# A fused embedding, SSM and mixture-of-experts block: row norms taken two tiles at a time, GpSimd work in smaller pieces, bias scaling on ScalarE

## The reference

```python
h = embed(ids) * 16                       # four tables, each with its projection to 256
x = layernorm(h)                          # over the 256 channels of a row
x1 = x @ w1.T + b1
xc = silu(depthwise_conv3(x1))            # along the sequence
y  = ssm(xc)                              # h = h*sigmoid(A) + x*B; y = sum(h*C) + D*x
h  = h + (y * silu(x @ v1.T + b2)) @ w2.T + b3
x = layernorm(h)
h = h + (shared_mlp(x) + mean of two hashed experts(x)) / 2
```

## Time and profile before

| | us |
|---|---|
| median of 3 runs | 460.0 (458.8 to 461.04) |
| the profiled execution, whole | 457.65 |
| its span in the profile | 455.8 |
| PE busy, DVE busy | 404.1, 292.9 |
| ACT busy, POOL busy | 240.3, 225.9 |
| stage A (start to first SSM matmul) | 0 to 141.8 |
| stage B (to the last toep slice) | 141.8 to 172 |

### The profile page before, as it was taken

One profiled execution on the slowest core, in us unless ns is written; L12 is line 12 of the kernel. 1 busy time (PEld: TensorE's weight loads), 2 busy tenths in 40 slices (PEclk: granted clock), 3 DMA queues, 4 the chain that ended last, 5 costly groups with the idle time before them and its releaser, 6 DMA issues.

```text
span 455.8 us, 8449 instructions
## 1 busy us (share of the span) xinstructions
PE 404.1 (89%) x2880; PEld 353.5 (78%) x2880; DVE 292.9 (64%) x624; ACT 240.3 (53%) x433; POOL 225.9 (50%) x242
## 2 busy tenths in 40 slices
PE   3778898999688777499899999999999999998996
PEld 3667776888467775278798898888988998987885
DVE  6678999978956568966555556375466465565333
ACT  4556776778477425553553654544535544534442
POOL 6787877952891007562834535535445337244000
PEclk9999999999899889789999999999999999999999
DMA  2324111139299997110130120130130121100101
GB/s 61 116 78 154 47 43 48 52 113 319 77 318 285 221 258 239 47 47 0 47 93 1 47 92 2 46 92 0 46 93 28 40 70 46 47 0 0 47 0 46
DMA packets 32619, 38.86 MB, mean 85 GB/s; under 512 B 3301, under 2 KB 28867, under 8 KB 32464
## 3 DMA queue, kind: packets, MB, share of 16 engines
q1 hardware_dynamic: 29456, 32.99, 24.8%
q0 software_dynamic: 3136, 5.52, 4.1%
HBM read 34.56 MB, written 8.65 MB: 95 GB/s over the span
## 4 chain that ended last, share of the span: by engine, by line
PE 63%; DVE 19%; issue 6%; ACT 5%; DMA 4%; POOL 1%; DVEq 0%; ACTq 0%; SPq 0%; POOLq 0%
PE ps L1128 19%; PE ps L1129 19%; PE ps L1130 19%; DVE hn L953 3%; DMA toep_l<-kernel_rows_dram 3%; DVE hid_lo L1059 3%; PE ps L1211 2%; DVE stat L940 2%; DVE catT_lo L933 1%; PE ps L1247 1%; DVE h2n L953 1%; DVE v_sb L1013 1%; DVE sw_lo L1006 1%; PE ps L1136 1%; PE ps L1166 1%
## 5 line engine op out<-in xcount | busy, mean ns | idle before, releaser
L1059 DVE SCALAR_TENSOR_TENSOR hid_lo<-act_out,hid_hi 128x512 fp32r<-128x512 f32 x64 | 54.5, 853 | 56.4 <-ACT hid_hi L847 56.4
L834 ACT ACTIVATE act_out<-ps,vec 128x512 f32<-128x512 f32 x32 | 22.0, 688 | 90.7 <-PE ps L1130 90.7
L533 POOL TENSOR_TENSOR rstd<-rstd,minus_half 128x1 f32<-128x1 f32 x64 | 40.5, 633 | 53.1 <-DVE rstd L949 52.5
L1053 DVE SCALAR_TENSOR_TENSOR act_out<-ps,vec,act_out 128x512 f32<-128x512 f32 x32 | 24.0, 751 | 55.5 <-ACT act_out L834 55.5
L666 POOL TENSOR_TENSOR h_sb<-h_sb,bias_e 128x256 f32<-128x256 f32 x32 | 24.3, 764 | 53.6 <-DVE h2n L953 53.6
L1129 PE MATMUL ps<-h2nT_lo,sw_hi 128*128 128x512 f32 x128 | 50.0, 391 | 0.0
L1130 PE MATMUL ps<-h2nT_hi,sw_lo 128*128 128x512 f32 x128 | 50.0, 391 | 0.0
L1128 PE MATMUL ps<-h2nT_hi,sw_hi 128*128 128x512 f32 x128 | 49.9, 390 | 0.0
L659 POOL TENSOR_TENSOR zc_lo<-v_sb,zc_hi 128x256 fp32r<-128x256 f32 x32 | 29.6, 924 | 36.7 <-ACT zc_hi L824 36.7
L838 ACT ACTIVATE act_out<-ps,vec 128x512 f32<-128x512 f32 x32 | 22.0, 688 | 41.6 <-PE ps L1130 41.4
L847 ACT ACTIVATE hid_hi<-act_out 128x512 fp32r<-128x512 f32 x64 | 39.7, 621 | 0.0
(11 more groups left out here) (131 smaller groups left out, 1278.8 us busy)
## 6 DMA issues: line engine op xcount, KB each, us to landing
toep_l<-kernel_rows_dram SPq DMA_DIRECT2D x6, 1024.0 KB, 11.7
h_rows_dram<-h_ring SPq DMA_DIRECT2D x32, 128.0 KB
toep_r<-kernel_rows_dram SPq DMA_DIRECT2D x4, 1024.0 KB, 7.0
h_in<-h_rows_dram SPq DMA_DIRECT2D x8, 512.0 KB, 4.4
stage<-w_e_dram POOLq DMA_DIRECT2D x7, 512.0 KB, 3.6
out_dram<-o_sb SPq DMA_DIRECT2D x7, 512.0 KB, 3.2
toep_r<-kernel_rows_dram SPq DMA_DIRECT2D x4, 512.0 KB, 9.5
bias_e<-rows_dram SPq DMA_DIRECT2D x1, 1024.0 KB, 7.5
```

Source lines behind the costliest of these rows:

```text
L533: nc.gpsimd.tensor_tensor(rstd[:, m:m + 1], rstd[:, m:m + 1], minus_half[:, :], ALU.pow).then_inc(s_rstd, 1)
L834: nc.scalar.activation(act_out[:, n % 4, :], ps[bank][:, :], ACT.Silu, bias=vec[:, C_SB1 + j:C_SB1 + j + 1]).then_inc(act_done, 1)
L1053: nc.vector.scalar_tensor_tensor(act_out[:, n % 4, :], ps[bank + 1][:, :], vec[:, C_SB3 + j:C_SB3 + j + 1], act_out[:, n % 4, :], ALU.add, ...
L1059: nc.vector.scalar_tensor_tensor(hid_lo[:, n % 4, :], act_out[:, n % 4, :], 0.5 if kind == SHARED else 0.25, f32(hid_hi[:, n % 4, :]), ALU ...
```

## The change

Four edits.

- `norm` is put in odd steps only, two tiles at once, right behind `cat` and ahead of the eviction of h (`emb`) and of `stats`. `eps` is put in even steps and adds 1e-5 in two columns of `rstd` with one instruction; POOL's `power_pair` raises two columns at once.
- The `kernel_step`s work on 256 elements of a partition instead of 512, two of them a step, in steps 9 to 23. The two `wv_lo` operations move from steps 4 and 6 to steps 8 and 9, and ACT's `wv_hi` from step 1 to step 5.
- The scaling of the biases moves from POOL (L631, L632) to ACT, ahead of the copies of slice q = 1 in stage B.
- POOL's bias additions wait for that (`bias_scaled`), so they run in stage B instead of at the end of stage A.

```diff
@@ phase_a
             behind("out", r, 1)
+            if r % 2:
+                add("norm", 0, r - 3) if r >= 3 else add("norm", 1, RES - 2)
+                add("norm", 0, r - 2) if r >= 3 else add("norm", 1, RES - 1)
             add("emb", 0, r - 1) if r else add("emb", 1, RES - 1)
             add("stats", 0, r - 1) if r else add("stats", 1, RES - 1)
-            add("norm", 0, r - 2) if r >= 2 else add("norm", 1, RES - 2 + r)
             add("aggr", 0, r - 1) if r else add("aggr", 1, RES - 1)
             behind("conv_left", r, 1, X1_AT)
-            add("eps", 0, r - 1) if r else add("eps", 1, RES - 1)
+            if r % 2 == 0:
+                add("eps", 0, r - 2) if r else add("eps", 1, RES - 2)
@@ POOL
+        def power_pair(n, m):
+            pool.wait_ge(eps_done, n // 2 + 1)
+            nc.gpsimd.tensor_tensor(rstd[:, m:m + 2], rstd[:, m:m + 2], minus_half[:, :].broadcast_to([P, 2]),
+                                    ALU.pow).then_inc(rstd_done, 2)
...
-            if n < 2:
-                double(5, 16 * n, 16)
-            elif n < 6:
-                double(6, 8 * (n - 2), 8)
-            elif n < 10:
-                fold((n - 6) // 2, 4 * ((n - 6) % 2), 4, 8)
+            if n < 4:
+                double(5, 8 * n, 8)
+            elif n < 12:
+                double(6, 4 * (n - 4), 4)
+            elif n < 20:
+                fold((n - 12) // 4, 2 * ((n - 12) % 4), 2, 8)
+            elif n < 24:
+                fold((n - 20) // 2, 2 * ((n - 20) % 2), 2, 4)
+            elif n < 26:
+                fold(n - 24, 0, 2, 2)
...
-                if r or i:
-                    power_step(RES * i + r - 1, (r - 1) % 4, eps_done, rstd_done)
+                if r % 2 == 0 and (r or i):
+                    power_pair(RES * i + r - 2, (r - 2) % 4)
...
-                if i == 0 and r in (4, 6):
+                if i == 1 and r < 2:
...
-                if 1 <= i <= 2:
-                    kernel_step(RES * (i - 1) + r)
+                if i == 1 and r or i == 2:
+                    kernel_step(2 * (RES * (i - 1) + r) - 2)
+                    kernel_step(2 * (RES * (i - 1) + r) - 1)
...
-        pool.wait_ge(rows_in, 32)
-        link(nc.gpsimd.tensor_scalar(bias_e[:, :, :], bias_e[:, :, :], 0.25, None, ALU.mult))
-        link(nc.gpsimd.tensor_scalar(bias_row[:, 0, :], bias_row[:, 0, :], 0.5, None, ALU.mult))
+        pool.wait_ge(bias_scaled, 2)
@@ ACT
-            if r == 1:
+            if r == 5:
                 act.wait_ge(wa_in, 32)
...
+            if q == 1:
+                act.wait_ge(rows_in, 32)
+                nc.scalar.mul(bias_row[:, 0, :], bias_row[:, 0, :], 0.5).then_inc(bias_scaled, 1)
+                nc.scalar.mul(bias_e[:, :, :].rearrange("p e c -> p (e c)"), bias_e[:, :, :].rearrange("p e c -> p (e c)"),
+                              0.25).then_inc(bias_scaled, 1)
@@ DVE
         def eps(i, r):
-            add_eps(RES * i + r, r % 4, aggr_done, eps_done)
+            m = r % 4
+            need(dve, aggr_done, RES * i + r + 2)
+            nc.vector.tensor_scalar(rstd[:, m:m + 2], mv[:, m:m + 2, 1], EPS, None, ALU.add).then_inc(eps_done, 1)
```

More of the change, by code:

```diff
@@ L187, in _tower @@
     k_out = sem("k_out")
+    bias_scaled = sem("bias_scaled")
     bias_step = sem("bias_step")
@@ L330, in _tower @@
     K_FIRST = 1 + 2 * 5 + 1
-    BIAS_STEPS = 3 + 2 * RES
+    BIAS_STEPS = 1 + 2 * RES
     def hn_bank():
@@ L553, in fold @@
                                            power[:, at + keep:at + keep + width, :], ALU.add))
-        def row_sum(half):
-            at = half * STATES
-            k_link(nc.gpsimd.tensor_tensor(k_sum[:, half, :], power[:, at, :], power[:, at + 1, :], ALU.add))
         def kernel_step(n):
+            halves = power[:, :, :].rearrange("p (h s) t -> p h s t", h=HALVES)
+            row_hi, row_lo = [k_row[:, SEQ - 1:2 * SEQ - 1, :, w].rearrange("p t c -> p c t") for w in range(2)]
             if n == 0:
@@ L565, in kernel_step @@
                 pool.wait_ge(k_pool, k_steps)
-            if n < 2:
-                double(5, 16 * n, 16)
-            elif n < 6:
-                double(6, 8 * (n - 2), 8)
-            elif n < 10:
-                fold((n - 6) // 2, 4 * ((n - 6) % 2), 4, 8)
-            elif n < 12:
-                fold(n - 10, 0, 4, 4)
-            elif n < 14:
-                fold(n - 12, 0, 2, 2)
-                pool.wait_ge(k_pool, k_steps)
-                row_sum(n - 12)
-            else:
-                row_hi, row_lo = [k_row[:, SEQ - 1:2 * SEQ - 1, :, w].rearrange("p t c -> p c t") for w in range(2)]
-                if n == 14:
-                    k_link(nc.gpsimd.tensor_tensor(k_sum[:, :, 0], k_sum[:, :, 0], vec[:, C_D:C_D + 2], ALU.add))
-                    pool.wait_ge(k_pool, k_steps)
-                    pool.wait_ge(row_zero, 1)
-                    k_link(nc.gpsimd.tensor_copy(row_hi, k_sum[:, :, :]))
-                else:
-                    k_link(nc.gpsimd.tensor_tensor(row_lo, k_sum[:, :, :], row_hi, ALU.subtract))
-                    pool.wait_ge(k_pool, k_steps)
-                    pool.dma_start(kernel_rows, k_row[:, :, :, :].rearrange("p n c w -> p (n c w)").bitcast(F32)
-                                   ).then_inc(k_out, 16)
@@ new lines, in kernel_step @@
+            if n < 4:
+                double(5, 8 * n, 8)
+            elif n < 12:
+                double(6, 4 * (n - 4), 4)
[5 more added lines that the diff above has]
+                fold(n - 24, 0, 2, 2)
+            elif n == 26:
+                k_link(nc.gpsimd.tensor_tensor(k_sum[:, :, :], halves[:, :, 0, :], halves[:, :, 1, :], ALU.add))
+            elif n == 27:
+                k_link(nc.gpsimd.tensor_tensor(k_sum[:, :, 0], k_sum[:, :, 0], vec[:, C_D:C_D + 2], ALU.add))
+            elif n == 28:
+                pool.wait_ge(row_zero, 1)
+                k_link(nc.gpsimd.tensor_copy(row_hi, k_sum[:, :, :]))
+            else:
+                k_link(nc.gpsimd.tensor_tensor(row_lo, k_sum[:, :, :], row_hi, ALU.subtract))
+                pool.wait_ge(k_pool, k_steps)
+                pool.dma_start(kernel_rows, k_row[:, :, :, :].rearrange("p n c w -> p (n c w)").bitcast(F32)
+                               ).then_inc(k_out, 16)
@@ L599, in group @@
                     gather(i + 1, r + LEAD - RES)
-                if i == 0 and r in (4, 6):
-                    m = (r - 4) // 2
+                if i == 1 and r < 2:
+                    m = r
                     pool.wait_ge(wa_hi, 2)
@@ L618, in _ @@
             group(i)
-        power_step(RES * GROUPS - 1, (RES - 1) % 4, eps_done, rstd_done)
+        power_pair(RES * GROUPS - 2, (RES - 2) % 4)
         steps = 0
```

## The result

| | before | after |
|---|---|---|
| median of the runs, us | 459.6 (458.8 to 461.0) | 447.8 (447.3 to 448.2) |
| profiled execution, us (its span) | 457.65 (455.8) | 447.28 (445.3) |
| step 11 / 22 / 31 of stage A starts | 38.57 / 82.09 / 111.02 | 35.74 / 75.55 / 104.89 |
| first `toep_l` issued | 123.63 | 112.43 |
| last `toep_l` landed | 169.38 | 158.84 |

The ratio of the times is 0.974 (95% interval 0.971 to 0.977). The forecast was 449.5, from a sum of 10.5 us on the profiled execution; that became 10.4 us shorter.

What follows compares the result with a forecast made beforehand. It took DVE, held by and chained to POOL, as the limit in steps 11 to 22 of stage A, transfers in stage B and PE in stage C; 460.0 - (5.0 + 4.0 + 1.5) = 449.5 us, range 446.5 to 452.5.

Steps and rivals of the forecast that it cites:

- The bias term: End of stage A: without POOL's 5.39 us scaling the last norm shortens and the stream starts 5.0 us earlier (4.4 to 5.5).
- the rival of 454.5: Stage B: bias additions come late, hold SP 5 us and delay stage C's first weights by up to that; chance 0.07.
- Steps 11 to 22: Stage A: a step takes 3.6 us instead of 3.96, gaining 4.0 us in eleven steps (bounds 0 and 8.2).
- Group 0: Early stage A: shift no longer waits beside wv_lo in steps 4 and 6, gaining 1.5 us (bounds -1.0 and 2.5).
- PE's own pace: Stage A, steps 22 to 31: 3.21 us a step once POOL no longer makes the taps, taken as PE's limit.
- The sum: Whole kernel: 5.0 + 4.0 + 1.5 = 10.5 us gained, median 449.5 us.
- The rule against the change: Stage A: two-column eps may take the port and wait up to 0.75 us for a POOL piece; result then 453.6.
- The price of 4.1 us: Stage A, steps 11 to 22: eps waiting up to 0.75 us in each of 5.5 pairs, all that the steps gain.
- PE's pace: Rival, steps 11 to 22: norms slip between short pieces, the steps gain all 8.2 us, giving 445.3; chance 0.13.

Runs made afterwards that it cites:

- e1: Changed kernel with POOL scaling the biases again at the end of stage A, the additions following it there; 454.6 us.
- e10: Changed kernel with ACT's bias scaling at q == 10 of the SSM stage instead of q == 1; 451.9 us.
- e4: Changed kernel with norm, eps and power one tile a step as before; short pieces and bias part kept; 451.1 us.
- e7: Kernel before with the pairs alone (norm, eps and power of two tiles), long pieces kept; 458.3 us.
- e8: Kernel before with the short pieces alone (256 elements, two a step, from step 9); 455.8 us.
- e5: Changed kernel with the two-column eps split into two additions of one column; 446.8 us.
- e6: Changed kernel with the V weights converted early again (ACT at step 1, POOL at steps 4 and 6); 448.0 us.
- e3: Changed kernel with tap pieces of 512 elements again, one a step from step 8; 455.7 us.
- e2: Kernel before with only the bias scaling moved to ACT and the additions to stage B; 455.5 us.
- e9: Changed kernel with 22 of 26 doublings and folds left out, the other four shortened (taps not the reference's); steps 13 to 22 took 29.67 us.

## Why the prediction was right, and where it was not

**The bias term**, 5.0 forecast, measured 5.07 between step 31 and `toep_l` and 5.10 by e1. Right in mechanism and size. The scaling on ACT took 1.93 + 0.44 us, forecast at most 2.5, and was covered: the stream kept 0.66 us in all. The additions came 3.5 us early instead of just in time, and e10 shows late ones to be cheap: 10.9 us of lateness cost some 3, where the rival of 454.5 took all of its 5 to the end.

**Steps 11 to 22**, 4.0 forecast (39.6 us), measured 3.71 (39.81). The number was right; the reason given first was wrong. "The norms leave the link from stats to eps, and POOL waits for DVE once in two steps" gains nothing by itself: e4 has the same steps without it, and with long pieces it loses (e7, 1.3 us), because POOL's one wait in two steps is 3.4 us long. What gains is the other half of that paragraph, that a norm "waits for a piece of 0.75, not of 1.29": e8 has 3.61 of the 3.71 us from it alone. I had not priced the two halves apart, so their sum hid that one of them was nothing. That the steps end where forecast is in this respect luck.

**Group 0**, 1.5 forecast within -1.0 to 2.5, measured 2.83, outside the bounds. The term that failed is "with `wv_lo` gone from steps 4 and 6 that is 2 to 3 x 0.85", and with it what stood against it: only that "a shift in step 9 can still meet `wv_lo`". The `shift` does get short (0.21 at most), and where nothing is held by the moved `wv_lo`, step 11 comes 1.1 us earlier (e5 at 34.45 against e6 at 35.52, which also differ in the form of `eps`) or 1.3 (e3 against e7). But in the changed kernel the moved `wv_lo` holds the `eps` of step 10 for 1.65 us, and in e6, with `wv_lo` back in place, step 11 starts as early. The 2.83 us come from elsewhere: e8 gets 1.63 from where the first pieces now stand, and e6 another 1.42 from the pairs, neither of which was in the term.

**Steps 22 to 31** weren't a term of the sum: "PE's own pace" left no room for loss. They lost 0.41 us: with the short pieces alone it is 1.23 (e8; twice as many pieces are left for these steps), and the pairs give 0.8 of it back (e8 30.16, e6 29.35).

**The sum** holds in another division, and its closeness is luck. Against the forecast group 0 gave 1.3 us more; steps 11 to 22 gave 0.3 less, steps 22 to 31 took 0.4 and the stream 0.7. The rest, 0.1 us, is the bias. Put in one after the other and read at step 31, where the bias can't act yet: short pieces 4.01 (e8), pairs on top of them 2.78 (e6), the late V weights -0.66 (after); then the bias, 5.07, which makes the 11.20 at `toep_l`. Such a reading is good to some 0.7 us: e10 differs from the changed kernel by 0.66 at step 31, and e2 from before by 0.31, with nothing changed ahead of it. So the -0.66 of the late V weights and the 0.55 that follows are not told from nothing, and the pairs' share is good to as much. The pairs give 1.24 alone (e7) and 2.78 behind short pieces, 1.42 of that in group 0 and only 0.55 in steps 11 to 22, where I had looked for it.

**The rule against the change.** The two-column `eps` did wait for POOL, five times in 16, up to 1.65 us. The Trainium skill, "VectorE: DVE Perf Modes", section "Mode 2×_2P — use both read ports for one tensor", lets an operation with a single input, in SBUF at both ends, use both read ports when its outermost dimension is even, and the two columns agree with that. It also lets an odd dimension through when it is the same at both ends, so it does not say that one column is spared, as I had read it; that one column is never held is what the rows show (the earlier trace rows and the 32 of e5). The price of 4.1 us that I derived fell: only three of the long ones are in steps 11 to 22, some 0.4 to 0.55 us over the rest each, and e5 shows no cost at step 31, since DVE waits there for POOL's power or the wait moves to the next operation.

**PE's pace** as a rival (445.3) was not reached. Its pace of 3.21 us a step was near (3.30 in steps 13 to 22 of e9), and so was the room that it names, but the change took only about half of it there: 3.94 us a step before, 3.60 after. The rest is what the short pieces still cost, 2.7 us in nine steps.

## What to carry to other kernels

Where DVE operations are held by whole GpSimd operations, cut the GpSimd operations before reordering DVE's: a cut to half cost 0.21 us of fixed time per piece and gave 3.6 us in eleven steps, while batching DVE's side behind long pieces made one long wait out of two short ones. When two parts of a change act on the same wait, price each with the other absent. Look at PE's granted clock in short stretches before two stretches are compared: four of the executions here had several microseconds at the lower clock in the very steps in question. A long GpSimd operation at a stage's seam costs its whole length if the next stage's start waits for a VectorE operation beside it.
